# Routed experts: gate and up rows on the partitions, 48-row rests side by side, copied up weights, three tables of sums

## The reference, cut to what matters

```python
topk_w, topk_ids = jax.lax.top_k(jax.nn.softmax(x @ gate_w.T), 4)
def body(acc, ew):
    w13_e, w2_e, e = ew                      # (352, 256), (256, 176)
    coef = jnp.sum(jnp.where(topk_ids == e, topk_w, 0.0), axis=-1)
    g, u = jnp.split(x @ w13_e.T, 2, axis=-1)
    return acc + ((silu(g) * u) @ w2_e.T) * coef[:, None], None
sparse_out, _ = jax.lax.scan(body, zeros, (w13, w2, jnp.arange(16)))
out = shared + sparse_out
```

## Time and profile before

| | us |
|---|---|
| median of 3 runs | 1282.1 (1281.39 to 1282.67) |
| the profiled execution, whole | 1278.6 |
| its span, first to last instruction | 1276.8 |
| PE busy in the span | 1195.4 |
| mean granted PE clock, share of full speed | 0.971 |

### The profile page before, as it was taken

One profiled execution on the slowest core, in us unless ns is written; L12 is line 12 of the kernel. 1 busy time (PEld: TensorE's weight loads), 2 busy tenths in 40 slices (PEclk: granted clock), 3 DMA queues, 4 the chain that ended last, 5 costly groups with the idle time before them and its releaser, 6 DMA issues.

```text
span 1276.8 us, 23433 instructions
## 1 busy us (share of the span) xinstructions
PE 1195.4 (94%) x7699; PEld 1029.2 (81%) x7700; DVE 830.1 (65%) x2038; ACT 739.2 (58%) x1606; POOL 621.3 (49%) x497
## 2 busy tenths in 40 slices
PE   6999999999984899997999999999999998779997
PEld 5888888888773677676899999999999987567775
DVE  7877777777782333368777777777777778333335
ACT  5756556555541233335888788888788875223332
POOL 3211222112127055542677777777777753715663
PEclk9999999999997799998999999999999999979999
DMA  3365665662236557761222222222222113666665
GB/s 114 85 188 154 173 171 162 167 165 66 63 122 222 172 98 125 139 144 34 71 63 72 72 63 69 58 58 63 60 65 82 34 46 96 230 190 108 115 114 144
DMA packets 94275, 141.56 MB, mean 111 GB/s; under 512 B 8184, under 2 KB 73976, under 8 KB 93048
## 3 DMA queue, kind: packets, MB, share of 16 engines
q1 hardware_dynamic: 74400, 102.32, 29.8%
q0 software_dynamic: 15744, 20.98, 9.5%
q10 hardware_dynamic: 4056, 17.30, 4.3%
HBM read 99.71 MB, written 40.86 MB: 110 GB/s over the span
## 4 chain that ended last, share of the span: by engine, by line
PE 76%; DMA 9%; DVE 6%; issue 5%; ACT 2%; POOL 1%; SPq 0%; DVEq 0%; POOLq 0%; ACTq 0%
PE ps L272 21%; PE ps L274 21%; PE ps L273 21%; DMA sums_d<-e_y,xg 7%; PE ps L1107 5%; PE ps L1132 3%; DMA rows_a<-a_rows_d 1%; DVE valT L753 1%; PE ps L561 1%; PE ps L1120 1%; PE ps L1084 1%; PE ps L338 1%; DVE ln_st L387 1%; DVE x L1406 1%; DMA sums<-sums_d 0%
## 5 line engine op out<-in xcount | busy, mean ns | idle before, releaser
L1278 POOL DMA_INDIRECT sums_d<-e_y,xg x88 | 137.6, 1563 | 146.2 <-ACT e_y L1209 95.6
L1107 PE MATMUL ps<-w,e_xT 128*128 (+1 forms) x376 | 127.5, 461 | 1.9 <-ACT e_xT L1192 1.0
L1399 DVE COPY e_hT<-ps 88x256 f32<-88x256 f32 x94 | 39.5, 421 | 130.6 <-PE ps L1120 116.3
L423 POOL TENSOR_TENSOR aw_lo<-aw_raw,aw_hi 128x512 fp32r<-128x512 f32 x32 | 42.1, 1318 | 157.6 <-ACT aw_hi L419 157.6
L847 DVE TENSOR_TENSOR m_a<-ps,e_a 128x384 f32<-128x384 f32 x128 | 71.3, 557 | 59.4 <-PE ps L274 58.7
L272 PE MATMUL ps<-xn_hi,aw_hi 128*128 128x512 f32 x256 | 107.3, 419 | 1.5 <-DVE bmat_lo L781 1.5
L274 PE MATMUL ps<-xn_hi,aw_lo 128*128 128x512 f32 x256 | 101.0, 395 | 0.0
L273 PE MATMUL ps<-xn_lo,aw_hi 128*128 128x512 f32 x256 | 100.6, 393 | 0.0
L423 POOL TENSOR_TENSOR qk_lo<-qf,qk_hi 128x512 fp32r<-128x512 f32 x64 | 84.3, 1338 | 26.2 <-ACT qk_hi L419 24.2
L1132 PE MATMUL ps<-w,e_hT 88*128 (+1 forms) x376 | 96.7, 379 | 0.0
L423 POOL TENSOR_TENSOR ms_b_lo<-m_b,ms_b_hi 128x384 fp32r<-128x384 f32 x64 | 65.1, 1018 | 47.9 <-ACT ms_b_hi L419 47.8
(11 more groups left out here) (303 smaller groups left out, 4206.2 us busy)
## 6 DMA issues: line engine op xcount, KB each, us to landing
rows_a<-a_rows_d SPq DMA_DIRECT2D x64, 256.0 KB, 5.1
xg<-slots_d SPq DMA_DIRECT2D x94, 144.0 KB
slots_d<-slot_init SPq DMA_DIRECT2D x10, 1152.0 KB, 6.7
w<-moe_up ACTq DMA_DIRECT2D x8, 1408.0 KB
wconv_raw<-b_conv SPq DMA_DIRECT2D x16, 513.0 KB
aw_raw<-a_heads SPq DMA_DIRECT2D x32, 256.0 KB, 3.0
wvo_raw<-b_vo SPq DMA_DIRECT2D x16, 512.0 KB
rows_b<-b_rows_d SPq DMA_DIRECT2D x32, 256.0 KB, 5.0
```

Source lines behind the costliest of these rows:

```text
L423: return nc.gpsimd.tensor_tensor(dst[1], src, f32(dst[0]), ALU.subtract).then_inc(sem(done_sem), 1)
L1107: ins = nc.tensor.matmul(ps[:, 2 + t % 2, 0:2 * E_HIDDEN], e_xT[:, t % 2, k], weights_of(w13, t, at_w, k * 2 * E_HIDDEN, 2 * E_HIDDEN), st ...
L1278: nc.gpsimd.indirect_dma_start(sums_d[f][t % CHAINS], bass.IndirectOffsetOnAxis(ap=xg[:, t % XG, ROW_ID:ROW_ID + 1].bitcast(U32), axis=0), ...
L1399: nc.vector.tensor_copy(e_hT[0:HALF_E, t % 2], ps[0:HALF_E, 4 + t % 2, 0:2 * P].rearrange("p (j m) -> p j m", j=2)).then_inc(sem("e_hT"), 1)
```

## The change

- `e_up_pe`: the weights are now the stationary operand and `e_xT` the moving one, so the hidden units lie on the partitions and h needs no turn before the down product. The 352 rows are cut in three blocks: 128 gate rows, 128 up rows, and 48 gate and 48 up rows in one block of 112 (the up ones from row 64). That is six matmuls of 128 moving columns instead of two of 352.
- The turns of `e_h` and the copies to `e_hT` are gone. ACT takes two silus a tile, DVE two products: 128 rows into `h_main`, 48 rows into `h_rest`, at partitions 0 to 47 for even tiles and 64 to 111 for odd ones. The coefficient moves into the scale of ACT's `e_y` copy.
- `e_down_pe` takes a group of tiles (`DOWN_GROUPS`: nine of four, five of two, one of one), two tiles behind up: first all 48-row rests, then all 128-row parts, each tile in a bank of its own.
- From tile 16 on DVE copies the tile's up weights to `w_more` (two buffers, 128 x 736) and, for odd tiles, the rest of its down weights to `w_rest`. DVE now loads the registers for these, PE those for the down products.
- `e_ids` and `coef` are kept for all tiles, so that `xg` is free after its turn; `e_y` has eight buffers; there are three tables of sums and three chains. e_last(0) to (2) follow the last down product. The tables' init, load and add come three times instead of two.

```diff
+DOWN_GROUPS = [range(t, t + 4) for t in range(0, 36, 4)] + [range(t, t + 2) for t in range(36, TILES - 1, 2)] + [range(TILES - 1, TILES)]
+DOWN_LAG = 2
-XG, YS, CHAINS, W_GROUPS = 8, 4, 2, 4
+XG, YS, CHAINS, W_GROUPS, HT = 8, 8, 3, 4, 6
...
+        def due(t):
+
+            return [g for g in DOWN_GROUPS if min(g[-1] + DOWN_LAG, TILES - 1) == t]
+
         def f_experts_pe(pe, f):
 
-            at_w = [None] * 3
-            for t in range(-1, TILES + 2):
+            e_turn_pe(pe, f, 0)
+            for t in range(TILES):
                 if t + 1 < TILES:
                     e_turn_pe(pe, f, t + 1)
...
+                if t == EXPERTS:
+                    routed(pe, "dve", f, "w_at")
+                e_up_pe(pe, f, t)
+                for group in due(t):
+                    e_down_pe(pe, f, group)
+            for i in range(LAST):
                 e_last_pe(pe, f, i)
...
+        def up_weights(t, first, n):
 
             if t < EXPERTS:
...
+                return w13[:, t * E_UP + first:t * E_UP + first + n]
+            return w_more[:, t % 2, first:first + n]
+
+        def down_weights(pe, t):
+
+            r = rest_rows(t)
+            if t < EXPERTS:
+                return w2[:, t * E_DOWN:t * E_DOWN + DM], w2[r, t * E_DOWN + DM:(t + 1) * E_DOWN]
+            e_at = expert_at(pe, t, 1)
+            return w2[:, bass.ds(e_at, DM)], w_rest[r, t // 2 % (HT // 2)] if t % 2 else w2[r, DM:][:, bass.ds(e_at, DM)]
...
+        def e_up_pe(pe, f, t):
 
             pe.wait_ge(sem("e_xT"), TILES * f + t + 1)
+            if t >= EXPERTS:
+                pe.wait_ge(sem("w_more"), MORE_TILES * f + t - EXPERTS + 1)
             if t >= 2:
                 pe.wait_ge(sem("e_h"), TILES * f + t - 1)
...
-            for k in range(KT):
-                ins = nc.tensor.matmul(ps[:, 2 + t % 2, 0:2 * E_HIDDEN], e_xT[:, t % 2, k],
-                                       weights_of(w13, t, at_w, k * 2 * E_HIDDEN, 2 * E_HIDDEN),
-                                       start=k == 0, stop=k == KT - 1, skip_group_check=True)
+            for first, n in UP_BLOCKS:
+                for k in range(KT):
+                    ins = nc.tensor.matmul(ps[0:n, 2 + t % 2, first:first + P], up_weights(t, k * E_WIDE + first, n),
+                                           e_xT[:, t % 2, k], start=first == 0 and k == 0, stop=k == KT - 1, skip_group_check=True)
             ins.then_inc(sem("e_up"), 1)
...
+        def e_down_pe(pe, f, group):
+
+            weights = [down_weights(pe, t) for t in group]
+            pe.wait_ge(sem("e_h"), TILES * f + group[-1] + 1)
...
+            for t, w in zip(group, weights):
+                rows_in = rest_rows(t)
+                nc.tensor.matmul(ps[:, 4 + t % 4, 0:DM], h_rest[rows_in, t // 2 % (HT // 2)], w[1],
+                                 start=True, stop=False, skip_group_check=True)
+            for t, w in zip(group, weights):
+                nc.tensor.matmul(ps[:, 4 + t % 4, 0:DM], h_main[:, t % HT], w[0],
+                                 start=False, stop=True, skip_group_check=True).then_inc(sem("e_down"), 1)
...
+            e_row_dve(dve, f, 0)
+            for t in range(TILES):
+                if t + 1 < TILES:
+                    e_row_dve(dve, f, t + 1)
+                if EXPERTS <= t + 1 < TILES:
+                    e_weights_dve(dve, f, t + 1)
+                e_h_dve(dve, f, t)
...
+        def e_weights_dve(dve, f, t):
+
...
+            else:
+                dve.wait_ge(sem("e_up"), TILES * f + t - 1)
+            if t % 2:
+                if t - HT >= EXPERTS:
+                    dve.wait_ge(sem("e_down"), TILES * f + t - HT + 1)
+                r = rest_rows(t)
+                nc.vector.tensor_copy(w_rest[r, t // 2 % (HT // 2)], w2[r, DM:][:, bass.ds(expert_at(dve, t, 1), DM)])
+            nc.vector.tensor_copy(w_more[:, t % 2], w13[:, bass.ds(expert_at(dve, t, 0), E_UP)]).then_inc(sem("w_more"), 1)
...
                 if t >= XG:
-                    added(sp, f, t - XG)
+                    sp.wait_ge(sem("e_row"), TILES * f + t - XG + 1)
+                    sp.wait_ge(sem("e_turned"), TILES * f + t - XG + 1)
```

More of the change, by code:

```diff
@@ L1124, in e_down_pe @@
[L1124 to L1135 removed]
+            elif group[-1] >= 4:
+                pe.wait_ge(sem("e_y"), TILES * f + group[-1] - 3)
@@ L1204, in e_y_act @@
             if t >= POOLED:
-                nc.scalar.copy(y_last[0][:, t - POOLED], ps[:, 6 + t % 2, 0:DM]).then_inc(sem("e_y"), 1)
+                nc.scalar.activation(y_last[0][:, t - POOLED], ps[:, 4 + t % 4, 0:DM], ACT.Copy, scale=coef[:, t:t + 1]
+                                     ).then_inc(sem("e_y"), 1)
                 return
@@ L1208, in e_y_act @@
                 added(act, f, t - YS)
-            nc.scalar.copy(e_y[:, t % YS], ps[:, 6 + t % 2, 0:DM]).then_inc(sem("e_y"), 1)
+            nc.scalar.activation(e_y[:, t % YS], ps[:, 4 + t % 4, 0:DM], ACT.Copy, scale=coef[:, t:t + 1]).then_inc(sem("e_y"), 1)
         CHAIN = [len(range(q, POOLED, CHAINS)) for q in range(CHAINS)]
@@ new lines, in e_weights_dve @@
+        def e_weights_dve(dve, f, t):
+            if t == EXPERTS:
+                routed(dve, "dve", f, "w_at")
+                for g in range(W_GROUPS):
+                    dve.wait_ge(sem(f"w_loaded{g}"), 32 * (f + 1))
+            else:
+                dve.wait_ge(sem("e_up"), TILES * f + t - 1)
[5 more added lines that the diff above has]
+            nc.vector.tensor_copy(w_more[:, t % 2], w13[:, bass.ds(expert_at(dve, t, 0), E_UP)]).then_inc(sem("w_more"), 1)
@@ L2198, in _ @@
             f_dve(dve, 3, 1)
-            for c in range(CHUNKS):
-                f_last_dve(dve, 3, 1, 0, c)
+            for i in range(CHAINS - 1):
+                for c in range(CHUNKS):
+                    f_last_dve(dve, 3, 1, i, c)
             for c in range(CHUNKS):
```

173 lines of the change are left out of this document (75 added, 98 removed).

## The result

| | before | after |
|---|---|---|
| median, us | 1281.4 (1279.5 to 1282.7) | 1309.9 (1305.8 to 1313.1) |
| ratio | 1 | 1.0233, 95% interval 1.0207 to 1.026 |
| profiled execution: span, us | 1276.8 | 1311.2 |
| mean granted PE clock | 0.971 | 0.959 |

The change makes the kernel slower by 2.3%. The forecast was 1.5% (1301.1). The page of the kernel after: span, busy time, the granted clock in 40 slices, and the group of the up passes with the idle time in front of them.

A forecast was written before the change was run, and what follows sets the result against it. PE's passes were taken to bound each routed stage (47 x 2.49 = 117 us). A stage: -3.3 - 0.82 x 5 + 9.0 + 8.5 + 0 + 0.3 = +10.4; two 20.8 - 1.8 = +19.0, median 1301.1, range 1266 to 1313.

The forecast's parts named there:

- group of four before tile 16: Routed stages, first 16 tiles: four tiles take 9.14 us instead of 9.96, -0.82 a group, -3.3 a stage.
- waits for w_more in a run of four: Tiles 14 to 37: PE waits for DVE's weight copies, 1.5 us a run of four ups, +9.0 a stage.
- PE stands for the four loads: Tiles 16 to 35: four register loads in a row before a group stop PE 1.7 us, five times, +8.5 a stage.
- two xg stalls of before, both stages: At 520.23 and 536.29: PE's stalls go as xg buffers no longer wait for adds, 0.9 each, -1.8 in all.
- pairs, 36 on: Tiles 36 to 46: -0.21 a pair by the passes, about as much lost to loads that stick out: 0.
- tail: End of a stage: the third table's sum starts in what was a wait for y_last, +0.3 a stage.
- Up part: Up passes: twelve of 0.11 us, 1.32 against 1.19, +0.13 a tile.
- Down part: Down products: e_h turns go, -0.22 a tile; rests overlap fully, 0.43 a pair; array shape change 0.40 a group.
- rival 1: Tiles 16 on: copies and loads are hidden, -16.0, so 1266.1 us; chance 0.16.
- until up(t) is issued: Before a group from tile 16: 0.35 us added to four loads' 2.6, with 0.1 for the first address.
- Rivals 2 and 3: 2: the loads alone count, DVE's chain fits, 1283.1, chance 0.14. 3: the rests do not overlap, 1320.9, chance 0.06.
- Rival 4: Copies cost more (0.92 each, about 4 us) and adds reach POOL in bursts (4 to 8 us): 1307; chance 0.06.

The follow-up runs named there:

- e4: Changed kernel without PE's register loads or DVE's loads and copies, all 48-row rests on partitions 0 to 47 so none share the array; ratio 1.0080 to before.
- e2: Changed kernel with up weights and odd tiles' down rests at constant places from tile 16, no DVE register loads or copies; ratio 1.0022 to before.
- e6: Changed kernel with all its work, w_more with three buffers, xg with six, up weights copied one tile earlier; ratio 1.0153 to before.
- e1: Changed kernel with PE's down weights at constant places from tile 16, so no register loads on PE; DVE's copies stay; ratio 1.0087 to before.
- e5: Changed kernel with all its work, PE's down register loaded right behind each up instead of four in a row; ratio 1.0056 to before.
- e7: As b3, but the third table is neither loaded back nor summed; ratio 0.9940 to before.
- b3: Changed kernel, one PE load behind each up, three w_more buffers copied for t + 3 behind h(t), w_rest copied during PE's groups; ratio 0.9955 to before.
- e8: Kernel before with three tables and three chains of adds, nothing else changed; ratio 1.0026 to before.
- e9: Changed kernel with all its work, one line changed: down products in groups of two throughout, no groups of four; ratio 0.9970 to before.
- e3: Changed kernel with no register loads on PE, no loads or copies on DVE, constant places for weights from tile 16; ratio 0.9933 to before.
- b1: Changed kernel with all its work, one PE load behind each up, three w_more buffers filled one tile earlier; ratio 1.0010 to before.

## Why the prediction was right, and where its sizes were off

It forecast slower, by two new waits in the tiles 16 to 35; both are there and nearly as large as worked out. That 1309.9 lies inside the range of 1266 to 1313 is in part luck: it is 3 us below the upper end, and what filled the distance, the tails and the clock, had no term of its size in the sum.

| step, a stage | predicted | measured |
|---|---|---|
| group of four before tile 16 | 9.14 (-0.82) | 9.46 (-0.50) |
| waits for w_more in a run of four | 1.5 | 0.51 + 0.77 = 1.3, of which ACT's 0.27 would be there without them |
| PE stands for the four loads | 1.7 | 3.09 - 1.42 = 1.67 |
| two xg stalls of before, both stages | -1.8 | -3.4 |
| pairs, 36 on | 0 | the last two pairs together +2.0 and +1.4 |
| low clock behind the gaps | not in it | +1.5 and +5.2 |
| tail | +0.3 | +2.9 and +4.9 |

- **Up part.** Passes 0.11 apart, as taken from the turns; 1.33 for twelve.
- **Down part.** Full overlap, shown by e4. The change of the array's shape costs 0.40 a group: the last up to the rests 0.20 instead of 0.11, rests 1.06 instead of 0.86, the 128-row parts 1.84 instead of 1.72 (461.77, 462.83 and 464.67 above). By the rule of the page "TensorEngine Tiling (Array Packing)" of the Trainium skill, section Key Properties, a change of mode drains the engine; the trace agrees for 48 rows, at these 0.40 a group.
- **The term missed in it** was ACT's order: four `e_y` at once delay two `e_xT`, 0.27 behind each of eight groups, 2.2 a stage. The prediction had compared ACT's busy time with PE's, which says nothing of a burst.
- **The copies.** The chain was right in its parts (copy 0.53 for 0.60, silus 0.56 for 0.5), and e2 and e6 show it from both sides. In the last pairs DVE makes the 0/1 matrices of `to_token` beside the copies, and the ups wait for a late `w_more` (the one at 559.87 for a copy that ended at 559.77); without the copies (e2) or with them a tile earlier (e6) the lateness is gone. The prediction had set the pairs at 0.
- **The register loads.** 0.65 each (single steps up to 0.90), four in a row, and right in size. No row stands behind the 0.35 "until up(t) is issued" and the 0.1 "for the first address"; in the group shown 0.17 pass before the first load and 0.3 between the last one and the rests, so their sum was right. e1 and e5 show that the loads alone hold the group. By the page "TensorE: Matmul & The Clock Gate" of the Trainium skill, Part 1, PE has a queue of 64, and rival 1 hung on that. No run here shows how long the queue is. What mattered is that the register loads did not run ahead: in the ten groups the first one starts 0.06 to 0.17 behind the start of the last up, whose wait it stands behind, and 0.41 ahead of it where that wait is gone (e2).
- **The tail** is the term that failed, 0.3 forecast and 2.9 and 4.9 measured. The step was that the new table's sum "starts in what was a wait for y_last". The tables are not there by then: the last add is issued 2.4 us later against PE's end than before, and lands later still, since the loads of the other tables run beside it (e7 against b3). e8 prices the sum alone, in the kernel before: 2.66 in the second tail, 1.8 in the first. That the add is issued later fits the new order, in which the last down products come in pairs and in front of all three e_last; no run took that apart, but groups of four are not needed for it, as e9 has the same tails (13.9 and 9.5).
- **The clock** was in no rival. The four groups that took 7.7 to 7.9 us where the others took 6.0 to 6.5 make 6.7 us, over both stages.
- **The two old xg stalls** (-1.8): against a steady 2.49 the ups of the kernel before lose 2.7 in the first stage and 0.7 in the second, so the term should have been -3.4. The kernel after has none of these, but e8 keeps one (two ups 3.8 and 3.2 behind the one before, around tile 36 of the first stage) with three tables. So it is not the tables that remove them. That it is the earlier freeing of `xg`, as the prediction had it, fits, but no run did that alone.
- **Rival 1** (hidden copies and loads, 1266.1) is what e3 built: bodies of 118.0, 15.2 less than before in both stages together, where the rival had 14.8 and 1.8 for the stalls. Its tails, 8.3 longer where the rival had 0.6, made it 1272.3 beside 1280.4. Rivals 2 and 3 are excluded, by the waits for `w_more` and by e4. Rival 4's dearer copy is as well, at 0.53; its other half, adds that come to POOL in bursts for 4 to 8 us, has the size of what the tails did (7.2 more than forecast), but not by groups of four, as e9 shows.

Put together: forecast +19.0, measured +34.4 in the profiled execution. Of the 15.4 between them 7.2 are the tails, 6.7 the clock, and 1.7 lie outside the routed stages; that is all of it, so the smaller rows above balance.

## What to carry to other kernels

A step that is cheap beside one tile's matmuls is not cheap four times in a row: count what the sequencer and the helper engines must do between two ups inside a burst, not on the mean over a stage. Here a group of four saved 0.12 us over two groups of two (9.46 against 9.58) and cost 2.7 us in waits; groups of two (e9), or register loads behind each up with copies further ahead and in b3's order, turn the same change from 2.3% slower into 0.3 to 0.5% faster; with the loads and copies moved but not reordered (b1) it is no gain (1.0010). And a table more in the tail costs its whole sum unless something there is shown to wait for something else, and its load can hold up the last add.

## What the runs showed of the hardware

- A releaser in a profile may be a coincidence: the loads ended at 518.3, the named product at 518.29, and e1 told them apart.
- After a gap in which PE was busy for 1.61 of 3.40 us, the granted clock was 0.68 for the next 4 us of full work; behind one just like it (1.76 of 3.30) it stayed at 1.00. Four of the ten later groups were hit; why those was not settled. With gaps of 2.4 to 2.9 (e2) none of ten was hit, with 2.9 to 3.3 (e6) one of ten, and with the gap gone (e1, e5, b3, e9) no group of the later tiles ran slow.
- One and the same kernel (before) took 1280.4, 1274.5 and 1231 to 1232 us on three chips, at granted clocks of 0.966 to 0.975, 0.965 to 0.975 and 0.986 to 0.994. On the last of them a wait shows that the others hide: PE comes to the routed stage before POOL has filled `slots_d`.
- An add issued by POOL had landed after 3.9 us where one other table of 1 MB was being loaded (e7, both stages), and after 7.0 and 9.4 us where two were (b3), by the start of the load that waits for it. The kernel before has 3.9 twice with one, e8 7.1 and 7.4 with two.
- Two matmuls of 48 rows at rows 0 and 64 start within 12 ns of each other (518.60 and 518.61) and cost together what one costs.
